# LSTM recurrence: products that stream their columns many times into unread PSUM

## The chip, the cores and the metric
One NeuronCore of a Trainium2 chip runs the whole kernel. The metric is the device time of one execution in microseconds. The kernel before took a median of 13971.03 us over 3 runs (13965.97 to 13977.05).

## What is computed
A graph network layer and a linear attention mix are added to x (6250 rows of 256); the result is normalised and goes through an LSTM with 256 state elements over all 6250 rows in order, batch 1. The part that the change touches is the LSTM:

```python
x_proj = jnp.einsum('btd,gd->btg', x, W_ih) + b_ih + b_hh
def step(carry, xp):
    h, c = carry
    gates = xp + h @ W_hh.T
    i, f, g, o = jnp.split(gates, 4, axis=-1)
    c = jax.nn.sigmoid(f) * c + jax.nn.sigmoid(i) * jnp.tanh(g)
    h = jax.nn.sigmoid(o) * jnp.tanh(c)
    return ((h, c), h)
```

Each step needs the state of the step before it, so the 6250 steps form one dependent chain.

## The kernel before
The kernel is a sequence of stages, each a block with one program for each engine. A normalisation of x, then a stage that gathers and scatters rows of the graph while TensorE computes the attention mix, then the feed-forward part of the graph network, its normalisation (products at lines 1161, 1170 and 1179), the recurrence (lines 1343 to 1564), and a last stage of running sums and output. The change is in the recurrence alone.

In the recurrence the 1024 gate rows are eight blocks of 128. Three gates (input, forget, cell) have two blocks each, m = 0 and 1, and collect in the PSUM regions gi[m][b]; the output gates collect in go[b]. b is one of two sets of banks: blocks of B = 5 steps alternate between them. So a region holds 5 steps, and for each step 3 gates with PARTS = 2 columns, 30 columns of the 512 of its bank, or 10 columns for the output gates. State, inputs and weights are split in two f16 parts each, so that three products (first part by first, first by second, second by first) replace one in f32. Each product is one load of 128x128 f16 weights (LDWEIGHTS) and one MATMUL with a moving operand of 1, 2, 5 or 10 columns.

TensorE's program of one step, in its order (`body`, from line 1434):
- `rest_of_weights`: 12 products of the weights' second parts with the state's first part, one column each. It waits for h1_ready of each half of the state.
- `weights` for m = 0: six products of the weights' first parts with both parts of the state, two columns, behind h2_ready of each half. The last signals ifg_made[0]. Then six for m = 1, and ifg_made[1].
- `output_gates`: 12 products of one column, then ogate_made.
- nine (or what is left) of the 44 products of `projection`, the input's share of the gates of the next five steps, written to the other set of banks. They have 5 or 10 columns: 6 x 5 for input, forget and cell gates and 2 x 7 for the output gates, the bias among them.


The other engines follow in a ring. VectorE sums the two parts of the gates (line 1538, once for each m), ScalarE takes tanh of them (line 1500, twice) and of the output gates (line 1505), VectorE makes the new cell (line 1542), ScalarE its tanh (line 1509), and VectorE writes the state's first part (line 1553, signals h1_ready) and its second (line 1558, h2_ready). Each engine works through its own queue in order; semaphores alone tie them together. SyncE moves the inputs in and the states out once in five steps. All products are issued by the helper at line 1422, so every one of them stands at that line in the profile:

```python
def matmul(to, w, v, start):
    return nc.tensor.matmul(to, w, v, start=start, stop=True, skip_group_check=True)
```

Of the kernel before, what the change touches and what calls it, by code (L numbers as in the profile page):

```python
# [33 lines left out]
KD = D // 128  # L34
# [18 lines left out]
B = 5  # L53
NB = N // B
NI = NB // 2
PARTS = 2
# [14 lines left out]
def due(count):  # L71


    return not isinstance(count, int) or count > 0
# [24 lines left out]
def gps_layer_kernel(nc, x, src, dst, gnn_eps, gW1, gb1, gW2, gb2, gamma, beta, w_qkv, b_qkv,  # L99
# [14 lines left out]
    with top, stage, nc.allow_non_contiguous_dma(reason="vectors of 256 numbers, loaded once"):  # L114
# [3 lines left out]
        def sb(name, shape, dt=F32, ctx=top):  # L118
            return ctx.enter_context(nc.sbuf_tensor(name, shape, dt))
# [6 lines left out]
        bank = [top.enter_context(nc.psum_tensor(f"bank{i}", [128, 512], F32)) for i in range(6)]  # L126
# [7 lines left out]
        whh = sb("whh", [128, PARTS, KD, G4], F16)  # L134
        wih = sb("wih", [128, PARTS, KD, G4], F16)
        gbias = sb("gbias", [128, G4], BF16)
# [30 lines left out]
        with ExitStack() as st:  # L167
# [15 lines left out]
            @block.sync  # L183
            def _(sp):
                xt, xnt = (v.rearrange("(p t) d -> p t d", p=R) for v in (x, xn_d))
                for j in range(XL):
                    at = slice(j * NT // XL, (j + 1) * NT // XL)
                    for lo, hi in SPLIT:
                        sp.dma_start(xall[lo:hi, at, :], xt[lo:hi, at, :]).then_inc(x_in[j], 16)
                for g in range(2):  # L190
                    for m, v in enumerate((src_g, dst_g)):
                        sp.dma_start(staged_i[:, g, m, :], v[g]).then_inc(staged[g], 16)
                sp.wait_ge(zeroed, 1)
                flat = [acc_d[a].rearrange("n d -> (n d)").rearrange("(p w) -> p w", p=128) for a in range(NA)]

                pieces = iter(range(NA * ZS))

                def zeros(count):
                    for _, piece in zip(range(count), pieces):
                        a, j = piece // ZS, piece % ZS  # L200
                        sp.dma_start(flat[a][:, j * ZW:(j + 1) * ZW], zero[:]).then_inc(zero_out[a], 16)

                zeros(ZEROS_AHEAD)
                for q in range(STORES):
                    at = slice(q * NT // STORES, (q + 1) * NT // STORES)
                    sp.wait_ge(xn_ready, (q + 1) * NT // STORES)
                    for lo, hi in SPLIT:
                        sp.dma_start(xnt[lo:hi, at, :], xall[lo:hi, at, :]).then_inc(xn_out, 16)
                    zeros(ZEROS_BETWEEN)
                zeros(NA * ZS - ZEROS_AHEAD - ZEROS_BETWEEN * STORES)  # L210
                sp.dma_start(x2_d[:, NB * KD * B * PARTS:], zero[:].bitcast(F16)[:, 0:2 * KD * B * PARTS]).then_inc(zero_out[NA - 1], 16)
                sp.wait_ge(xn_out, 32 * STORES)
# [1132 lines left out]
        with ExitStack() as st:  # L1345
            ones = sb("ones", [128, B], BF16, st)
            xs_ = sb("xsteps", [128, 2, PARTS, KD, B], F16, st)
            hp = sb("hp", [128, 2 * B, KD, 4], F16, st)
# [8 lines left out]
            gi = [[bank[2 * k + b][:, 0:B * 3 * PARTS].rearrange("p (t g c) -> p t g c", t=B, c=PARTS)  # L1357
                   for b in range(2)] for k in range(KD)]
            go = [bank[4 + b][:, 0:B * KD].rearrange("p (t m) -> p t m", t=B) for b in range(2)]

            def pair(name):
                return [sem(f"{name}{k}") for k in range(KD)]
# [12 lines left out]
            def steps(engine, body):  # L1375

                def blocks(i):
                    for b in range(2):
                        for s in range(B):
                            body(i * (2 * B) + (b * B + s), i, b, s)  # L1380

                first_apart(engine, NI, blocks)
# [20 lines left out]
            def projection(b):  # L1403

                for g in range(4):
                    for m in range(KD):
                        cols = slice((KD * g + m) * 128, (KD * g + m + 1) * 128)
                        if g == 3:
                            yield go[b][:, :, m], gbias[:, cols], ones[:], m == 0
                            for p, q in ((0, 0), (0, 1), (1, 0)):  # L1410
                                for k in range(KD):
                                    yield go[b][:, :, m], wih[:, p, k, cols], xs_[:, b, q, k, :], False
                        else:
                            to = gi[m][b][:, :, g, :]
                            yield to[:, :, 0:1], gbias[:, cols], ones[:].rearrange("p (t c) -> p t c", c=1), g == 0
                            for p in range(PARTS):
                                for k in range(KD):
                                    yield (to[:, :, 0:PARTS - p], wih[:, p, k, cols],
                                           xs_[:, b, 0:PARTS - p, k, :].rearrange("p c t -> p t c"), False)

            def matmul(to, w, v, start):
                return nc.tensor.matmul(to, w, v, start=start, stop=True, skip_group_check=True)  # L1422

            @block.tensor
            def _(pe):
                pe.wait_ge(lstm0, 1)
                pe.wait_ge(xs_in[0], 16)
                for m in projection(0):
                    last = matmul(*m)
                last.then_inc(x_proj, 1)  # L1430
                per_step = -(-(3 * KD * (1 + PARTS * KD) + KD * (1 + 3 * KD)) // B)
                state = {}

                def body(t, i, b, s):
                    if s == 0:
                        state["ahead"] = list(projection(1 - b))
                        pe.wait_ge(xs_in[1 - b], 16 * (i + 1 + b))
                    before = (b * B + s - 1) % (2 * B)

                    def product(to, p, k, g, m, at):  # L1440
                        cols = slice((KD * g + m) * 128, (KD * g + m + 1) * 128)
                        return matmul(to, whh[:, p, k, cols], hp[:, before, k, at], False)

                    FIRST, REST, BOTH = slice(3, 4), slice(2, 3), slice(2, 4)

                    def rest_of_weights(m, k):
                        for g in range(3):
                            product(gi[m][b][:, s, g, 0:1], 1, k, g, m, FIRST)

                    def weights(m, k):  # L1450
                        for g in range(3):
                            last = product(gi[m][b][:, s, g, :], 0, k, g, m, BOTH)
                        return last

                    def output_gates():
                        for m in range(KD):
                            to = go[b][:, s, m:m + 1]
                            for k in range(KD):
                                product(to, 1, k, 3, m, FIRST)
                                product(to, 0, k, 3, m, FIRST)  # L1460
                                last = product(to, 0, k, 3, m, REST)
                        return last

                    if due(t):
                        pe.wait_ge(h1_ready[0], t)
                    rest_of_weights(0, 0)
                    rest_of_weights(1, 0)
                    if due(t):
                        pe.wait_ge(h1_ready[1], t)
                    rest_of_weights(0, 1)  # L1470
                    rest_of_weights(1, 1)
                    if due(t):
                        pe.wait_ge(h2_ready[0], t)
                    weights(0, 0)
                    if due(t):
                        pe.wait_ge(h2_ready[1], t)
                    weights(0, 1).then_inc(ifg_made[0], 1)
                    weights(1, 0)
                    weights(1, 1).then_inc(ifg_made[1], 1)
                    output_gates().then_inc(o_made_, 1)  # L1480

                    n = per_step if s < B - 1 else len(state["ahead"])
                    for m in state["ahead"][:n]:
                        last = matmul(*m)
                    state["ahead"] = state["ahead"][n:]
                    if s == B - 1:
                        last.then_inc(x_proj, 1)

                steps(pe, body)

            @block.scalar
# [310 lines left out]
```

## Time and profile before

| | us |
|---|---|
| median of 3 runs | 13971.03 |
| profiled execution, its own time | 13987.69 |
| span of the profile | 13985.9 |
| TensorE busy with products | 10063.6 (72%) |
| TensorE busy with weight loads | 9131.5 (65%) |
| VectorE busy | 8604.1 (62%) |
| ScalarE busy | 5184.4 (37%) |
| mean granted clock of TensorE | 0.549 |

A busy share is the union of the records of an engine. A product's record lasts some 0.17 us, while the next one can start much earlier, so many overlap and a busy TensorE is not one at its peak. The granted clock is given as a share of 2.4 GHz: it has two levels, 1.0 and 0.5 (1.2 GHz). Times are in microseconds from the start of the span, except where a row gives a mean duration, which is in nanoseconds.

### The profile page before, as it was taken

The numbers are of one execution on the slowest core, as the hardware profiler recorded it, in microseconds if no ns is written. First come the engines' busy times: TensorE is split into PE (matmuls) and PEld (weight loads), VectorE is DVE, ScalarE is ACT, GpSimd is POOL, SyncE is SP. The second block draws the span as 40 slices with busy tenths as digits, with TensorE's granted clock in tenths as the row PEclk, the third lists the DMA queues.
The fourth block names the chain that finished last, engine by engine and source line by source line (L and its number), as shares of the span: only waits on it lengthen the run. The fifth ranks groups of instructions, "written<-read, shape, count | busy, mean of one in ns | idle before, by whom it ended". The sixth has DMA issues, their size and how long they took to land. (4 is left out here: it accounts for less than half of the span.)

```text
span 13985.9 us, 721250 instructions
## 1 busy us (share of the span) xinstructions
PE 10063.6 (72%) x285273; PEld 9131.5 (65%) x285273; DVE 8604.1 (62%) x65379; ACT 5184.4 (37%) x32393; POOL 2070.5 (15%) x1598
## 2 busy tenths in 40 slices
PE   3444444687777777777777777777777777777776
PEld 2333333567777777777777777777777777777775
DVE  4444222256666666666666666666666666666667
ACT  1111111144444444444444444444444444444443
POOL 5888788400000000000000000000000000000000
PEclk8666777865555555555555555555555555555556
DMA  6555455410000000000000000000000000000001
GB/s 164 91 90 90 80 83 83 92 34 1 1 1 1 1 1 1 1 1 1 1 1 1 1 1 1 1 1 1 1 1 1 1 1 1 1 1 1 1 1 19
DMA packets 2057504, 301.47 MB, mean 22 GB/s; under 512 B 1894943, under 2 KB 2013747, under 8 KB 2056843
## 3 DMA queue, kind: packets, MB, share of 16 engines
q0 software_dynamic: 150048, 204.90, 9.0%
q1 hardware_dynamic: 1896678, 91.09, 8.1%
q10 hardware_dynamic: 10742, 5.06, 0.1%
q8 instruction: 16, 0.26, 0.0%
q14 instruction: 20, 0.16, 0.0%
HBM read 153.07 MB, written 141.27 MB: 21 GB/s over the span
## 5 line engine op out<-in xcount | busy, mean ns | idle before, releaser
L1422 PE MATMUL bank<-hp,whh 128*128 128x1 f16 (+1 forms) x225000 | 7000.0, 166 | 2320.7 <-DVE hp L1553 2320.7
L1422 PEld LDWEIGHTS bank<-hp,whh 128*128 128x128 f16 x225000 | 6488.6, 104 | 2864.1 <-DVE hp L1553 2863.6
L1500 ACT ACTIVATE gates<-last_banks 128x3 f32<-128x3 f32 x12500 | 2085.4, 174 | 6161.2 <-DVE last_banks L1538 6161.2
L1538 DVE TENSOR_REDUCE last_banks<-bank 128x3 f32<-128x6 f32 x12500 | 2076.6, 172 | 2393.9 <-PE bank L1422 2393.9
L1422 PE MATMUL bank<-xsteps,wih 128*128 128x10 f16 (+1 forms) x45036 | 2331.0, 170 | 0.0
L1542 DVE CUSTOM_DVE_ANT_1 uv<-gates 128x4 f32<-128x4 f32 x12500 | 2019.4, 164 | 506.3 <-ACT gates L1500 0.2
L1553 DVE TENSOR_TENSOR_SCAN hp<-last_banks,opening 128x2 f16<-128x2 f32 x12500 | 1968.9, 161 | 569.1 <-ACT last_banks L1509 108.7
L1509 ACT ACTIVATE last_banks<-gates 128x1 f32<-128x1 f32 x12500 | 2085.2, 174 | 0.1
L1422 PEld LDWEIGHTS bank<-xsteps,wih 128*128 128x128 f16 x45036 | 1917.6, 104 | 0.0
L1558 DVE TENSOR_TENSOR_SCAN hp<-last_banks,hp 128x2 f16<-128x2 f32 x12500 | 1759.2, 159 | 0.0
L1629 POOL TENSOR_TENSOR U<-U (+1 forms) x25 | 27.5, 1139 | 11171.2 <-POOLq L1572 11171.2
L1422 PE MATMUL bank<-ones,gbias 128*128 128x5 bf16 x10008 | 1551.1, 168 | 9.4 <-DMA xsteps<-x_d 9.4
L385 POOL DMA_INDIRECT acc_d<-sums,target x782 | 1267.1, 1620 | 252.9 <-issue 204.7
L407 PE MATMUL bank<-rows,equal 128*128 128x256 f32 x1564 | 694.2, 622 | 778.0 <-DMA rows<-xn_d,staged_i 734.5
L407 PEld LDWEIGHTS bank<-rows,equal 128*128 128x128 f32 x1564 | 480.8, 322 | 927.3 <-issue 826.4
L1422 PEld LDWEIGHTS bank<-ones,gbias 128*128 128x128 bf16 x10008 | 1040.8, 104 | 9.7 <-issue 9.7
L1542 DVE DVE_READ_ACCUMULATOR2_ANT gates<- 128x1 f32 x12500 | 1038.5, 83 | 0.0
L1505 ACT ACTIVATE last_banks<-bank 128x2 f32<-128x2 f32 x6250 | 981.2, 157 | 0.0
L360 POOL DMA_INDIRECT rows<-xn_d,staged_i x782 | 774.7, 991 | 249.3 <-issue 215.9
L418 ACT ACTIVATE sums<-bank 128x512 f32<-128x512 f32 x391 | 212.1, 594 | 1587.2 <-PE bank L407 1583.0
L457 DVE TENSOR_TENSOR target<-dstf,move 128x4 int32<-128x4 f32 x196 | 32.0, 163 | 880.6 <-DMA acc_d<-sums,target 874.0
L644 PE MATMUL bank<-kvn 125*128 125x128 f32 x200 | 61.1, 461 | 482.7 <-DVE kvn L750 464.8
(184 smaller groups left out, 3199.8 us busy)
## 6 DMA issues: line engine op xcount, KB each, us to landing
xsteps<-x_d SPq DMA_DIRECT2D x1252, 5.0 KB, 1.8
U<-hp SPq DMA_DIRECT2D x1250, 5.0 KB, 2.5
acc_d<-zero SPq DMA_DIRECT2D x30, 640.0 KB, 12.9
ht<-acc_d SPq DMA_DIRECT2D x75, 224.0 KB
rows<-xn_d,staged_i POOLq DMA_INDIRECT x782
acc_d<-sums,target POOLq DMA_INDIRECT x782, 3.8
xi<-xn_d SPq DMA_DIRECT2D x50, 125.0 KB
xi<-in_x SPq DMA_DIRECT2D x50, 125.0 KB
```

The costliest lines, as they stand in the source:

```text
L360: pool.indirect_dma_start(out=rows[0:P, g, j, :], out_offset=None, in_=xn_d, in_offset=bass.IndirectOffsetOnAxis(ap=staged_i[0:P, g, 0, j: ...
L385: pool.indirect_dma_start(out=acc_d[a], out_offset=bass.IndirectOffsetOnAxis(ap=target[0:P, g, j:j + 1], axis=0), in_=sums[0:P, g, j, :], ...
L407: last = nc.tensor.matmul(prod[j // 2][0:P, j % 2, :], equal[0:P, g, j, 0:P], rows[0:P, g, j, :], start=True, stop=True)
L418: nc.scalar.activation(sums[0:P, g, 2 * m:2 * m + 2, :], prod[m][0:P], ACT.Copy)\
L1422: return nc.tensor.matmul(to, w, v, start=start, stop=True, skip_group_check=True)
L1500: nc.scalar.activation(gates[:, k, 0:6:2], zi[k], ACT.Tanh, scale=down)\
L1505: nc.scalar.activation(o_all, go[b][:, s], ACT.Tanh, scale=down).then_inc(o_act, 1)
L1509: nc.scalar.activation(o_tc[k][:, 1:2], gates[:, k, 5:6], ACT.Tanh).then_inc(tc_ready[k], 1)
L1538: nc.vector.tensor_reduce(zi[k], gi[k][b][:, s], axis=AX.X, op=ALU.add).then_inc(ifg_summed[k], 1)
L1542: nc.vector.tensor_tensor_reduce(out=uv[:, k, :].rearrange("p (a c) -> p a c", a=2), in0=gates[:, k, 0:4].rearrange("p (a c) -> p a c", a= ...
L1553: nc.vector.tensor_tensor_scan(hp[:, at, k, 2:4], o_tc[k], opening[:], RAISE, ALU.mult, ALU.subtract).then_inc(h1_ready[k], 1)
L1558: nc.vector.tensor_tensor_scan(hp[:, at, k, 0:3:2], o_tc[k], hp[:, at, k, 1:4:2], RAISE, ALU.mult, ALU.subtract).then_inc(h2_ready[k], 1)
```

## The change
Products write to wider regions. `gi_wide` and `go_wide` see the same banks as `gi` and `go`, but with the region repeated 16 times (30 columns each) and 48 times (10 columns each). Repetition 0 is what the other engines read, at the same place as before; the others are read by nobody. A product's moving operand is broadcast with a stride of zero, so that TensorE streams the same columns several times. The one-column products of `rest_of_weights` now have 16 columns, those of `weights` with k = 0 have 32 (with k = 1 still 2), those of `output_gates` 48, and those of `projection` 30. `spare_columns` is a product of 256 columns into the upper half of a bank of the set that is not being read; each step ends with two of them, and 48 precede step 0.

```diff
+            GATE_COLS, OUT_COLS = B * 3 * PARTS, B * KD
+            gi_wide = [[bank[2 * k + b][:, 0:GATE_COLS * 16].rearrange("p (j n) -> p j n", n=GATE_COLS) for b in range(2)]
+                       for k in range(KD)]
+            go_wide = [bank[4 + b][:, 0:OUT_COLS * 48].rearrange("p (j n) -> p j n", n=OUT_COLS) for b in range(2)]
+            NX = 6
+
+            def again(v, times):
+
+                return v.rearrange("p (o t) -> p o t", o=1).broadcast_to([128, times, v.shape[-1]])
...
-                            yield go[b][:, :, m], gbias[:, cols], ones[:], m == 0
+                            to = go_wide[b][:, 0:NX].rearrange("p j (t m) -> p j t m", m=KD)[:, :, :, m]
+                            yield to, gbias[:, cols], again(ones[:], NX), m == 0
...
-                                    yield go[b][:, :, m], wih[:, p, k, cols], xs_[:, b, q, k, :], False
+                                    yield to, wih[:, p, k, cols], again(xs_[:, b, q, k, :], NX), False
...
+                            to = gi_wide[m][b][:, 0:NX].rearrange("p j (t g c) -> p j t g c", g=3, c=PARTS)[:, :, :, g]
+                            yield to[:, :, :, 0], gbias[:, cols], again(ones[:], NX), g == 0
+                            for k in range(KD):
+                                both = xs_[:, b, 0:PARTS, k, :].rearrange("p c (o t) -> p o t c", o=1)
+                                yield (to[:, 0:NX // 2], wih[:, 0, k, cols],
+                                       both.broadcast_to([128, NX // 2, B, PARTS]), False)
+                            for k in range(KD):
+                                yield to[:, :, :, 0], wih[:, 1, k, cols], again(xs_[:, b, 0, k, :], NX), False
...
+                def spare_columns(b, start=False):
+
+                    return matmul(bank[2 + b][:, 256:512], wih[:, 0, 0, 0:128], whh[:, 0, 0, 0:256], start)
+
+                for n in range(48):
+                    spare_columns(1, start=n == 0)
...
-                        return matmul(to, whh[:, p, k, cols], hp[:, before, k, at], False)
+                        v = hp[:, before, k, at]
+                        return matmul(to, whh[:, p, k, cols], again(v, to.shape[1]) if len(to.shape) == 3 else v, False)
...
-                            product(gi[m][b][:, s, g, 0:1], 1, k, g, m, FIRST)
+                            product(gi_wide[m][b][:, :, col(s, g):col(s, g) + 1], 1, k, g, m, FIRST)
...
-                            last = product(gi[m][b][:, s, g, :], 0, k, g, m, BOTH)
+                            to = gi[m][b][:, s, g, :] if k else gi_wide[m][b][:, :, col(s, g):col(s, g) + PARTS]
+                            last = product(to, 0, k, g, m, BOTH)
...
-                            to = go[b][:, s, m:m + 1]
+                            to = go_wide[b][:, :, s * KD + m:s * KD + m + 1]
...
+                    for _ in range(2):
+                        last = spare_columns(1 - b)
```

TensorE, one step of the recurrence as it stood before (hp and whh are state and recurrent weights, xsteps and wih inputs and theirs, ones and gbias the bias):

```order
L1422 MATMUL bank<-hp,whh 128x1 x12
L1422 MATMUL bank<-hp,whh 128x2 x12
L1422 MATMUL bank<-hp,whh 128x1 x12
L1422 MATMUL bank<-xsteps,wih 128x5
L1422 MATMUL bank<-ones,gbias 128x5
L1422 MATMUL bank<-xsteps,wih 128x5 x6
```

TensorE, the same step after the change (the helper stands at line 1434 there):

```order
L1434 MATMUL bank<-hp,whh 128x16 x12
L1434 MATMUL bank<-hp,whh 128x16x2 x3
L1434 MATMUL bank<-hp,whh 128x2 x3
L1434 MATMUL bank<-hp,whh 128x16x2 x3
L1434 MATMUL bank<-hp,whh 128x2 x3
L1434 MATMUL bank<-hp,whh 128x48 x12
L1434 MATMUL bank<-xsteps,wih 128x30
L1434 MATMUL bank<-ones,gbias 128x30
L1434 MATMUL bank<-xsteps,wih 128x30 x6
L1434 MATMUL bank<-whh,wih 128x256 x2
```

The 36 products with the state keep their order; the two of 256 columns are the last of the step, ahead of the next step's first product in the queue.

## Rows read from the trace of the kernel before

**Rows 1.** The page: span, and the granted clock in 40 slices.
```profile
span 13985.9 us, 721250 instructions
...
PEclk8666777865555555555555555555555555555556
```

**Rows 2.** Stretches of stages: length, busy time and count by engine, granted clock.
```profile
core 0: us, PE busy (x) PEld busy (x) DVE busy (x) ACT busy (x) POOL busy (x), PEclk, DMA share, GB/s
2700.00:2860.00 160.00, 158.99 (x793) 141.66 (x793) 60.89 (x108) 54.76 (x132) 0.00 (x0) 1.00 0.31 93
2900.00:2985.00 85.00, 74.90 (x242) 53.89 (x242) 53.63 (x153) 42.59 (x83) 0.00 (x0) 0.50 0.14 52
...
5000.00:13000.00 8000.00, 6283.69 (x207033) 5881.75 (x207030) 5438.31 (x46215) 3446.91 (x23110) 0.00 (x0) 0.50 0.08 1
```

**Rows 3.** Waits of the recurrence, 5000 to 13000: us in total, times, longest.
```profile
DVE last_banks L1538 <- PE bank L1422: 1766.5, 4621, 0.4
PE bank L1422 <- DVE hp L1553: 1716.1, 4621, 0.5
```

**Rows 4.** Groups by form, 5000 to 13000: busy us, mean ns, idle before.
```profile
L1422 PE MATMUL bank<-hp,whh 128*128 128x1 f16 x110908 | 4336.3, 166 | 1716.1 <-DVE hp L1553 1716.1
...
L1553 DVE TENSOR_TENSOR_SCAN hp<-last_banks,opening 128x2 f16<-128x2 f32 x9243 | 1455.9, 161 | 420.8 <-ACT last_banks L1509 80.4
...
L1422 PE MATMUL bank<-xsteps,wih 128*128 128x10 f16 x11089 | 1057.6, 172 | 0.0
```

**Rows 5.** Timeline of one step: start us, us, engine, line, operation.
```profile
8000.12 0.16 ACT L1505 ACTIVATE last_banks<-bank 128x2 f32<-128x2 f32 x1
...
8000.26 0.33 ACT L1509 ACTIVATE last_banks<-gates 128x1 f32<-128x1 f32 x2
...
8000.47 0.32 DVE L1553 TENSOR_TENSOR_SCAN hp<-last_banks,opening 128x2 f16<-128x2 f32 x2
8000.68 1.04 PEld L1422 LDWEIGHTS bank<-hp,whh 128*128 128x128 f16 x36 [0.45 <-DVE hp L1553]
8000.69 1.12 PE L1422 MATMUL bank<-hp,whh 128*128 128x1 f16 x36 [0.36 <-DVE hp L1553]
8000.70 0.28 DVE L1558 TENSOR_TENSOR_SCAN hp<-last_banks,hp 128x2 f16<-128x2 f32 x2
8001.37 0.33 DVE L1538 TENSOR_REDUCE last_banks<-bank 128x3 f32<-128x6 f32 x2 [0.38 <-PE bank L1422]
```

**Rows 6.** Timeline, line 1170: eight one-column products, at clock 1.0, at 0.5.
```profile
2872.11 1.09 PE L1170 MATMUL bank<-small,csq 128*125 128x1 f32 x8
...
2879.39 1.84 PE L1170 MATMUL bank<-small,csq 128*125 128x1 f32 x8
```

**Rows 7.** Groups by form on TensorE: at clock 1.0, then at 0.5.
```profile
L1063 PE MATMUL bank<-hid,gw 128*128 128x250 f32 x364 | 80.8, 374 | 1.0 <-ACT U L1093 1.0
...
L1042 PE MATMUL bank<-ident,hsum 125*128 125x125 f32 x84 | 12.5, 270 | 0.0
...
L1170 PE MATMUL bank<-small,csq 128*125 128x1 f32 x8 | 1.1, 257 | 0.0
...
L1170 PE MATMUL bank<-small,csq 128*125 128x1 f32 x140 | 32.3, 351 | 0.1
L1179 PE MATMUL bank<-ident,nrs 125*128 125x125 f32 x34 | 11.2, 432 | 0.0
```

**Rows 8.** Scatter stage: a timeline piece, then stretches, columns as in rows 2.
```profile
332.60 3.55 PE L407 MATMUL bank<-rows,equal 128*128 128x256 f32 x8 [2.05 <-issue]
...
322.60:329.40 6.80, 3.34 (x19) 2.36 (x18) 2.58 (x6) 2.45 (x7) 5.27 (x6) 1.00 0.71 122
329.40:332.80 3.40, 1.35 (x7) 0.72 (x6) 3.19 (x8) 0.00 (x0) 2.90 (x2) 1.00 0.28 83
332.80:336.20 3.40, 3.36 (x8) 2.10 (x7) 2.70 (x5) 0.64 (x2) 2.99 (x2) 0.50 0.68 65
336.20:339.60 3.40, 0.00 (x0) 0.00 (x0) 0.00 (x0) 1.08 (x2) 2.79 (x3) 1.00 0.61 65
```

More of the change, by code:

```diff
@@ L1408, in projection @@
                         if g == 3:
-                            yield go[b][:, :, m], gbias[:, cols], ones[:], m == 0
+                            to = go_wide[b][:, 0:NX].rearrange("p j (t m) -> p j t m", m=KD)[:, :, :, m]
+                            yield to, gbias[:, cols], again(ones[:], NX), m == 0
                             for p, q in ((0, 0), (0, 1), (1, 0)):
                                 for k in range(KD):
-                                    yield go[b][:, :, m], wih[:, p, k, cols], xs_[:, b, q, k, :], False
+                                    yield to, wih[:, p, k, cols], again(xs_[:, b, q, k, :], NX), False
                         else:
[L1414 to L1419, printed above, removed]
+                            to = gi_wide[m][b][:, 0:NX].rearrange("p j (t g c) -> p j t g c", g=3, c=PARTS)[:, :, :, g]
[6 more added lines that the diff above has]
+                                yield to[:, :, :, 0], wih[:, 1, k, cols], again(xs_[:, b, 0, k, :], NX), False
             def matmul(to, w, v, start):
@@ L1441, in product, with col @@
                         cols = slice((KD * g + m) * 128, (KD * g + m + 1) * 128)
-                        return matmul(to, whh[:, p, k, cols], hp[:, before, k, at], False)
+                        v = hp[:, before, k, at]
+                        return matmul(to, whh[:, p, k, cols], again(v, to.shape[1]) if len(to.shape) == 3 else v, False)
+                    def col(s, g):
+                        return (s * 3 + g) * PARTS
                     FIRST, REST, BOTH = slice(3, 4), slice(2, 3), slice(2, 4)
```

## The prediction
> **What bounds the kernel now.** The page is read first: the span, and the row of the granted clock [rows 1]. It averages 0.6 to 0.8 in the first nine slices and stands at 0.5 from the tenth to the end of the recurrence. That is the lower of the engine's two levels, 1.2 GHz, for three quarters of the span. Stretches by stage say it sharply [rows 2]: 5000 to 13000 us is one uniform stretch at 0.50. The scan of line 1553 runs twice a step and stands 9243 times in those 8000 us [rows 4], so a step takes 8000 / 4621.5 = 1.731 us, and the 6250 steps take 10.8 ms.
>
> The waits of that stretch [rows 3] show a ring with no engine full. VectorE waits for TensorE 1766.5 / 4621 = 0.38 us a step, and TensorE for VectorE 0.37 us. The timeline of one step gives the ring [rows 5]: scan at .47, first weight load at .68, first product at .69, first reduction at 1.37, and so on through VectorE and ScalarE to the next scan. Of its 1.731 us, 0.68 us (.69 to 1.37) is TensorE's: it is the time from the first product to the reduction that needs the 18th. The 36 products of the ring start within 1.12 - 0.166 us, so one follows another at 0.954 / 35 = 0.0273 us [rows 4, 5]. A product with 10 columns lasts 6 ns longer than one with 1, and its neighbours follow no later. So it is the load of 128x128 weights ahead of each product that sets this pace, not the columns.
>
> **The change, part by part.** A step has 104 columns now: 12 + 24 + 12 of the state, and 280 of the inputs spread over five steps. After it: 12x16 for the first parts, 2x(3x32 + 3x2) for both parts, 12x48 for the output gates, 264 for inputs (44 products of 30 columns over five steps), 512 for the two spare products. Together 1748. The number of products on the ring, their order and all waits stay. Added are two products and two loads at the end of each step, and 48 products before step 0. VectorE, ScalarE and SyncE get nothing new, and nothing they read gets wider.
>
> **Does the clock rise, and hold?** At 1.2 GHz a column takes 0.83 ns, so the new step would stream 1.45 us of columns, against 0.09 of 1.73 us now. What the trace shows of the clock: with 250-column products back to back the level was 1.0 [rows 2, 7]; with TensorE busy 88% of the time, but mostly on 1-column products, it was 0.50 [rows 2, 7], and it is 0.50 in the recurrence. So neither having records nor having no long gap is enough; streamed columns differ. The 48 products are 12,288 columns on end, and I expect 1.0 within them, as it rose in the scatter stage after a stretch at 0.5 in which products of 256 columns kept the engine busy for 3.36 of 3.40 us [rows 8]. Holding is the doubtful half. At 2.4 GHz the step streams 1748 x 0.417 ns = 0.73 us of about 1.65, 44%. In the scatter stage the level stayed at 1.0 over 6.80 us in which wide products kept the engine busy 3.34 us, and fell after a stretch with 1.35 us of 3.40 [rows 8]. The new step stands nearer to the first. I take it that it holds.
>
> **What a full clock is worth.** The nearest rows for the pace are one-column products with a full weight load at both levels [rows 6, 7]: eight in 1.84 us at 0.5 give (1.84 - 0.351) / 7 = 0.213 us each, eight in 1.09 us at 1.0 give (1.09 - 0.257) / 7 = 0.119. Ratio 0.56, so 0.0273 becomes 0.015 us. These loads are f32, ours f16; the other end is no gain, 0.0273. I take 0.015, because these rows too are set by the load. Seventeen such paces would save 0.21 us, but the ring has a second edge. The products with the new state's second half (the 16th on) wait for the scan pair of line 1558, which ends at .98 [rows 5]. From a scan's end to the load it releases are 0.05 us (.63 to .68 [rows 5]). So the 16th product can come at about 1.03 + 0.02 = 1.05, and now it comes at .69 + 15 x 0.0273 = 1.10. That gives 0.05 us, and the two paces after it 2 x 0.012 = 0.024: **0.075 us a step**.
>
> The time from a product's start to its result may fall too. For one column nothing does, once the pace is taken off: 0.351 - 0.213 = 0.138 and 0.257 - 0.119 = 0.138 [rows 6, 7]. For 125 columns, 432 ns at 0.5 and 270 at 1.0, columns taken off (208 and 104), 224 and 166 are left [rows 7]: 0.058 less, of which a part is the wait of the first of a pair, so I bound it by 0.05. The ring's products ahead of the reduction have two columns, nearest to one: I take 0, and keep 0.05 for the range. The Trainium skill ("TensorE: Matmul & The Clock Gate", "Single matmul latency") has a single product's latency fall from (219+N)/1.2 to (398+N)/2.4 ns; for N = 1 that is an estimated 17 ns, and the sum would be 106 us lower by it. The rows of one column show none of it.
>
> The second half of the gates gets its reduction six paces after the first, 0.09 for 0.16 us, but it follows VectorE and ScalarE behind the first half and sets nothing; I cost it at nothing. Widening at full clock costs nothing either: a 48-column product streams 0.020 us, its results are wanted by line 1505, which stands 0.14 us ahead of line 1509 in ScalarE's queue [rows 5]; 12 x 0.020 is still less than the 12 x 0.0273 it takes now. The two spare products take 512 x 0.417 = 0.21 us and lie in TensorE's idle 0.37 us. TensorE's own sum, 24 x 0.015 + 12 x 0.020 + 9 x 0.015 + 0.21 = 0.95 us, is far under the step, so its queue is empty when the scan comes. If that cover goes (at half clock), see the first rival. The 48 products cost between 48 x 0.107 = 5 and 48 x 0.213 = 10 us, once: 8.
>
> Sum: 6250 x 0.075 = 469, less 8, 461 us. The profiled execution took 13987.69 us (span 13985.9), the median of the runs is 16.7 us lower at 13971.03; the same difference is expected after. 13971 - 461 = **13510 us**.
>
> **Rivals.**
> The clock falls, or never rises (slower). The place is the output gates. At 1.2 GHz a 48-column product takes 0.040 us, not 0.0273: twelve end 0.15 us later, and their own columns add 0.04. Line 1505 comes 0.19 us later, and line 1509, which stands behind it on ScalarE and on the ring 0.14 us after it with a 0.16 us operation between [rows 5], comes about 0.17 later. TensorE alone gives a lower bound: 24 x 0.0273 + 12 x 0.040 + 9 x 0.0273 + 0.427 = 1.81 us, 0.08 more than the step. Per step +0.17: 6250 x 0.17 = 1060, **15030 us**. For it: 44% of columns is no dense stream, and 2900 to 2985 shows a busy engine at 0.5. Against it: at half clock the step would be filled with columns to 1.45 of 1.90 us, so a fall would tend to be followed by a rise. It decides from the point where a share f of steps at half clock has 0.17 f > 0.075 (1 - f): f over 0.31.
>
> The clock is full, but the pace hardly moves. Pairs of load and product then keep some 0.027 us, and what is left is 0 to 0.05 us a step of latency; the middle, 0.02, gives 6250 x 0.02 - 8 = 117 us less, **13854 us**. For it: no f16 load at 1.0 stands in this trace. Against it: the f32 rows. The Trainium skill states such a floor ("TensorE: Matmul & The Clock Gate", "Wait — 56ns, not 53.3ns?"): starts never closer than about 25 ns at full clock, however few the columns. By that page 17 x 0.0023 = 0.039 us a step would be saved, an estimate of 13735 us; the trace has 0.0273 at half clock and cannot show the floor.
>
> The change does not do what it says: the columns don't count as work for the clock, but the step has room for them. There is none at half clock (1.81 us against 1.731), so this ends in the first rival.
>
> **How the numbers follow.** Clock full and pace shortened: 0.52. Clock full and pace kept: 0.22. Clock at half for over a third of the steps: 0.20. Gain and loss about cancelling (f near 0.31): 0.06. A measurement here tells 0.2%, 28 us. The forecast's bounds are 0.125 us a step (0.075 + 0.05), which is 13971 - 781 + 8 = 13198, and about 0.05, 13665. The range goes from 13230 to 13900, to the far side of the second case, and leaves the slow case out. Faster 0.75: the first two cases, and a little of the last. Same 0.04, slower 0.21.
>
> **What would show it.** Right: PEclk 1.0 from 3000 us to the end; a step of 1.65 us; 36 ring products in 0.7 to 0.9 us instead of 1.12; VectorE's wait for TensorE 0.30 us a step instead of 0.38; the gaps between reduction, tanh, cell and scan unchanged. Pace kept: PEclk 1.0, but the first 18 products still in 0.46 us. Wrong: PEclk at 0.5 or mixed, line 1505's successor further from the reduction, and TensorE without idle time.

## The result, and the profile after

The changed kernel takes **14772.03 us** (median of 4 runs, 14764.79 to 14774.01) against 13969.15 of the kernel before in the same comparison: a ratio of 1.0573, 95% interval 1.0555 to 1.0591. It is 5.7% slower, 803 us. The forecast was 13510 us, faster, with a range to 13900.

The page of the changed kernel, its span, the granted clock, and one of its groups (busy us, mean ns, idle time before it and what ended it):

```profile
span 14771.7 us, 746346 instructions
...
PEclk8666777799999999999999999999999999999998
...
L1531 ACT ACTIVATE last_banks<-bank 128x2 f32<-128x2 f32 x6250 | 981.2, 157 | 1078.2 <-PE bank L1434 1078.2
```

The clock is what was forecast: 0.9 or more from the ninth slice to the last but one, where it was 0.5 from the tenth on [rows 1]. Stretches of it, columns as in [rows 2]:

```profile
3000.00:3010.00 10.00, 9.83 (x210) 8.65 (x209) 3.56 (x34) 2.19 (x17) 0.00 (x0) 1.00 0.01 2
...
5000.00:13000.00 8000.00, 7693.34 (x201653) 6494.99 (x201651) 4714.97 (x43090) 2812.12 (x21545) 0.00 (x0) 1.00 0.07 1
```

It is 1.00 from the first steps and for the whole recurrence, not 0.50. So the 803 us are lost at full clock.

The waits (us in total, times, longest) and the groups by form of the stretch from 5000 to 13000:

```profile
DVE last_banks L1564 <- PE bank L1434: 1825.1, 4309, 0.4
...
DVE hp L1579 <- ACT last_banks L1535: 1070.2, 4309, 0.3
ACT last_banks L1531 <- PE bank L1434: 743.3, 4309, 0.2
```

```profile
L1434 PE MATMUL bank<-hp,whh 128*128 128x48 f16 x51708 | 2983.1, 206 | 0.0
L1434 PE MATMUL bank<-hp,whh 128*128 128x16 f16 x51708 | 2071.2, 179 | 306.7
...
L1434 PE MATMUL bank<-hp,whh 128*128 128x2 f16 x25848 | 1563.8, 163 | 0.0
...
L1579 DVE TENSOR_TENSOR_SCAN hp<-last_banks,opening 128x2 f16<-128x2 f32 x8618 | 1085.3, 161 | 1070.2 <-ACT last_banks L1535 1070.2
```

The scan of line 1579 (1553 before) stands 8618 times, so a step takes 8000 / 4309 = 1.857 us, 0.1255 more than the 1.731 before; 6250 x 0.1255 = 784 us, which is the difference of the spans (14771.7 - 13985.9 = 785.8). Two waits of the table are new. ScalarE's line 1531 (1505 before), the tanh of the output gates, now waits 743.3 / 4309 = 0.17 us a step for TensorE, and the scan waits 1070.2 / 4309 = 0.25 us for ScalarE, where line 1553's wait was 80.4 us in all [rows 4]. The timeline of a step:

```profile
8001.48 1.32 PE L1434 MATMUL bank<-hp,whh 128*128 128x16 f16 x36
8002.14 0.32 DVE L1564 TENSOR_REDUCE last_banks<-bank 128x3 f32<-128x6 f32 x2 [0.42 <-PE bank L1434]
8002.34 0.32 ACT L1526 ACTIVATE gates<-last_banks 128x3 f32<-128x3 f32 x2 [1.02 <-DVE last_banks L1564]
...
8002.84 0.16 ACT L1531 ACTIVATE last_banks<-bank 128x2 f32<-128x2 f32 x1 [0.17 <-PE bank L1434]
...
8002.91 0.26 ACT L1535 ACTIVATE last_banks<-gates 128x1 f32<-128x1 f32 x2
8003.11 0.25 DVE L1579 TENSOR_TENSOR_SCAN hp<-last_banks,opening 128x2 f16<-128x2 f32 x2 [0.24 <-ACT last_banks L1535]
```

Set beside [rows 5]: from the first product to the first reduction it is 0.66 us (.48 to 2.14), 0.02 less than the 0.68 before. But the 36 products of the ring take 1.32 us instead of 1.12. Line 1531 starts at 2.84, 0.70 after the reduction; before, that was 0.48 (1.37 to 0.12 of the next step, 1.73 us on [rows 5]). Line 1535 (1509 before), the tanh of the cell, must follow it on ScalarE's queue and does so 0.07 us later. The ring loses there more than it wins at its start.

How much a 48-column product takes comes from the same row. The first 24 products need 24 x 0.0257 = 0.62 us (the reduction behind the 18th shows that pace: 0.66 less the 0.2 from a product's start to its reader is 0.46 for 18). The twelve of the output gates take the rest: 1.32 - 0.206 - 0.62 = 0.49 over 11 starts, **0.045 us each**, where I had put 0.020.

### The profile page after: what moved, and what is told of

Read it like the earlier page. It is cut to its first block and busy times, and to the rows that moved or that the text cites. A ratio compares the mean times of both kernels' runs of the same rounds, so it can differ in the third digit from the quotient of the medians.

```text
span 14771.7 us, 746346 instructions
## 1 busy us (share of the span) xinstructions
PE 12730.3 (86%) x297821; PEld 10604.7 (72%) x297821; DVE 8088.8 (55%) x65379; ACT 4602.0 (31%) x32393; POOL 2067.4 (14%) x1598
## 5 line engine op out<-in xcount | busy, mean ns | idle before, releaser
L1434 PEld LDWEIGHTS bank<-hp,whh 128*128 128x128 f16 x225000 | 7346.7, 96 | 2182.6 <-DVE hp L1579 2182.2
L1434 PE MATMUL bank<-hp,whh 128*128 128x16 f16 (+2 forms) x225000 | 8267.0, 185 | 444.7 <-DVE hp L1579 0.2
L1434 PE MATMUL bank<-xsteps,wih 128*128 128x30 f16 x45036 | 2506.8, 190 | 0.0
L1579 DVE TENSOR_TENSOR_SCAN hp<-last_banks,opening 128x2 f16<-128x2 f32 x12500 | 1574.1, 161 | 1552.2 <-ACT last_banks L1535 1552.2
L1434 PE MATMUL bank<-whh,wih 128*128 128x256 f16 x12548 | 2385.7, 272 | 0.0
L1434 PEld LDWEIGHTS bank<-xsteps,wih 128*128 128x128 f16 x45036 | 2007.1, 97 | 0.0
L1434 PE MATMUL bank<-ones,gbias 128*128 128x30 bf16 x10008 | 1712.6, 190 | 8.7 <-DMA xsteps<-x_d 8.7
L1535 ACT ACTIVATE last_banks<-gates 128x1 f32<-128x1 f32 x12500 | 1617.4, 167 | 0.0
L1584 DVE TENSOR_TENSOR_SCAN hp<-last_banks,hp 128x2 f16<-128x2 f32 x12500 | 1596.7, 164 | 0.0
L1434 PEld LDWEIGHTS bank<-whh,wih 128*128 128x128 f16 x12548 | 784.6, 97 | 1.2
```

Source lines behind the costliest of these rows:

```text
L1535: nc.scalar.activation(o_tc[k][:, 1:2], gates[:, k, 5:6], ACT.Tanh).then_inc(tc_ready[k], 1)
L1579: nc.vector.tensor_tensor_scan(hp[:, at, k, 2:4], o_tc[k], opening[:], RAISE, ALU.mult, ALU.subtract).then_inc(h1_ready[k], 1)
L1584: nc.vector.tensor_tensor_scan(hp[:, at, k, 0:3:2], o_tc[k], hp[:, at, k, 1:4:2], RAISE, ALU.mult, ALU.subtract).then_inc(h2_ready[k], 1)
```

## The experiments

Theory 1: the loss is the output gates' twelve products alone, because of something in how their 48 columns are read or written. Theory 2: it is spread, and goes with the number of columns a step streams, or with the spare products.

**What form of product is slow.** Twelve forms stand ahead of step 0, where the clock is already 1.0, twelve products of each on end, each with its own weight load. The number of columns is the label.

```diff
+                form(side[:, 0:40], whh[:, 0, 0, 0:40])
+                form(side[:, 0:44].rearrange("p (j n) -> p j n", n=1), again(state1, 44))
+                form(stepped(46), whh[:, 0, 0, 0:46].rearrange("p (j n) -> p j n", n=1))
+                form(stepped(48), again(state1, 48))
+                form(side[:, 0:42].rearrange("p (j n) -> p j n", n=1), whh[:, 0, 0, 0:42 * 4].rearrange("p (j n) -> p j n", n=4)[:, :, 0:1])
+                for n in (2, 8, 16, 24, 32):
+                    form(stepped(n), again(state1, n))
+                form(side[:, 0:24 * 10].rearrange("p (j n) -> p j n", n=10)[:, :, 0:2], again(whh[:, 0, 0, 0:2], 24))
+                form(side[:, 0:56], whh[:, 0, 0, 0:56])
```

(`stepped(n)` is n columns of PSUM that stand 10 apart, as in the changed kernel's output gates.)

> Eleven forms of product, twelve of each on end, stand after the 48 products and before step 0, at full clock. They tell whether the 44 ns from one 48-column product to the next come from reading one column over and over (stride 0) or from writing columns 10 apart. Theory 1, the read: 44 columns read with stride 0 and written side by side follow at about 0.93 x 44 = 41 ns, 46 columns read side by side and written apart at 25 ns or less. Theory 2, the write: the other way round, 25 and about 43 ns. 48 with both as in the changed kernel: 44 ns. 40 columns side by side on both: 25 ns, the floor that the two-column products show. Of the apart forms 2, 8, 16 and 24 columns 25 ns, 32 about 30 ns. 24 pairs (48 columns): under 30 ns if pairs move at full rate. The whole kernel: as the changed one, 14772 us plus about 5.

The whole kernel took 14778.08 us. Its groups by form, busy us and mean ns, from 3003.5 to 3008:

```profile
L1434 PE MATMUL bank<-whh,wih 128*128 128x46 f16 x12 | 0.7, 216 | 0.0
L1434 PE MATMUL bank<-whh,wih 128*128 128x44 f16 x12 | 0.6, 202 | 0.0
L1434 PE MATMUL bank<-whh,wih 128*128 128x42 f16 x12 | 0.6, 212 | 0.0
L1434 PE MATMUL bank<-whh,wih 128*128 128x32 f16 x12 | 0.5, 193 | 0.0
L1434 PE MATMUL bank<-whh,wih 128*128 128x24 f16 x12 | 0.5, 184 | 0.0
...
L1434 PE MATMUL bank<-whh,wih 128*128 128x40 f16 x12 | 0.5, 180 | 0.0
L1434 PE MATMUL bank<-whh,wih 128*128 128x56 f16 x11 | 0.4, 187 | 0.0
```

The stretch of the 24 pairs, and that of the 48 columns one by one:

```profile
L1434 PE MATMUL bank<-whh,wih 128*128 128x48 f16 x12 | 0.5, 183 | 0.0
```

```profile
L1434 PE MATMUL bank<-whh,wih 128*128 128x48 f16 x10 | 0.6, 208 | 0.0
```

A product of two columns lasts 163 ns in the ring at this clock, so the excess over it, divided by the number of columns, gives the price of a column. Columns side by side on both sides: 40 last 180 and 56 last 187, 0.43 ns each, the full rate. 24 pairs 10 apart: 183, 0.42. Forms whose columns are handled one by one: 44 last 202 (0.9), 46 last 216 (1.2), 48 last 208 (0.9), 42 last 212 (1.2), 24 last 184 (0.9). The ends of such records are modelled by the profiler; the starts are not, and they say the same. Products of 40 or 56 columns and of 24 pairs start 25 to 26 ns apart, those of 44, 46, 48 and 42 lone columns 41, 40, 45 and 39 ns, which is 0.9 ns a column throughout, and those of 8 to 24 lone columns 26.6 ns. Neither of my two theories on reading and writing held alone: 44 was written side by side and is slow, 46 was read side by side and is slow. But 44 and 46 both were given as rows of one element, so these forms leave open whether place or shape is what counts.

**Reading and writing apart.** Seven more forms, each with a plain single run where it can have one.

```diff
+                form(side[:, 0:50], state1.broadcast_to([128, 50]))
+                form(side[:, 0:52], apart(52, 2))
+                form(side[:, 0:54], apart(54, 8))
+                form(side[:, 0:2 * 36].rearrange("p (n j) -> p n j", j=2)[:, :, 0], many[:, 0:36])
+                form(side[:, 0:2 * 30].rearrange("p (j n) -> p j n", n=2), state1.rearrange("p (o t) -> p o t", o=1).broadcast_to([128, 30, 2]))
+                form(side[:, 0:2 * 31].rearrange("p (j n) -> p j n", n=2), again(many[:, 0:2], 31))
+                form(side[:, 0:58], many[:, 0:58])
```

> Seven more forms ahead of step 0, twelve products of each, at full clock, to split the reading side and the writing side. Durations over the 163 ns of a two-column product, per column: 0.43 ns is full rate, 0.9 or more is slow. If reading with stride 0 is slow in itself: 50 columns of one element with a single stride of 0 last 163 + 45 = 208 ns, and 60 columns of it written in pairs 217 or more. If only the shape (an inner run of one) was slow: 185 and 189. Columns read 2 elements apart (4 bytes), 52 of them: 185 if two in the same 16 bytes suffice, as the Trainium skill ('SBUF — State Buffer', 'Door 1: The DMA port swizzle') states; 210 if every column that is no neighbour is slow. 54 read 8 apart (16 bytes): slow, 212 or more. 36 columns written 2 apart (8 bytes), read side by side: slow, 163 + 36 x 1.15 = 204. 62 columns as 31 pairs: 190. 58 side by side: 188.

The whole kernel took 14769.46 us. Groups by form ahead of step 0:

```profile
L1434 PE MATMUL bank<-whh,wih 128*128 128x54 f16 x12 | 1.4, 278 | 0.0
L1434 PE MATMUL bank<-whh,wih 128*128 128x36 f16 x12 | 0.6, 201 | 0.0
L1434 PE MATMUL bank<-whh,wih 128*128 128x62 f16 x12 | 0.5, 191 | 0.0
L1434 PE MATMUL bank<-whh,wih 128*128 128x60 f16 x12 | 0.5, 191 | 0.0
L1434 PE MATMUL bank<-whh,wih 128*128 128x58 f16 x12 | 0.5, 188 | 0.0
L1434 PE MATMUL bank<-whh,wih 128*128 128x52 f16 x12 | 0.5, 186 | 0.0
L1434 PE MATMUL bank<-whh,wih 128*128 128x50 f16 x12 | 0.5, 183 | 0.0
```

Reading one element over and over is not slow: 50 columns of it last 183 ns and 60 last 191, close to the full rate. So the 44 of the kernel above were slow by their shape, a pattern whose inner run is one element, though the addresses were adjacent. Both their sides had that shape; which of the two counts was not tested. Reading 2 elements apart costs nothing (52 last 186), as the Trainium skill ("SBUF — State Buffer", "Door 1: The DMA port swizzle") has it for two hits on 16 bytes; reading 16 bytes apart costs most (54 last 278, and start 98 ns apart, 1.8 ns a column). Writing is the other half: 36 columns written 2 apart last 201 with a plain read, and start 34 ns apart, 0.94 ns each. The Trainium skill says so for PSUM ("PSUM — Partial Sum Buffer", "Specifications (TRN2)"): its lines are 8 bytes, two f32 values, and any non-contiguous pattern slows products. Lone columns at half the rate agree with it. The pairs do not: they too are non-contiguous, and go at full rate; there the measurement decides. The changed kernel's output gates had both faults, copies 10 apart and rows of one.

**The output gates narrow.**

```diff
-                            to = go_wide[b][:, :, s * KD + m:s * KD + m + 1]
+                            to = go[b][:, s, m:m + 1]
```

> The output gates' twelve products take one column again, all else as changed (1184 columns a step). Theory 1, they alone are the loss: if the clock holds at 1.0, the step is 1.731 - 0.024 = 1.707 us and the time about 13830; if it falls to 0.5, TensorE needs 45 x 0.027 + 0.43 = 1.63 us, just under the old step, and the time is 13980 to 14100. Theory 2, the loss is spread (spare products in the way, slower access to PSUM): over 14300 at clock 1.0.

13899.61 us, ratio to before 0.9946 (0.9930 to 0.9963). One line turns 803 us of loss into 72 us of gain: theory 1, and not theory 2, since the two spare products, the 16- and 32-column products and the wide inputs are all still there. Stretches, columns as in [rows 2]:

```profile
3000.00:3100.00 100.00, 91.16 (x2702) 75.09 (x2701) 65.35 (x570) 41.17 (x285) 0.00 (x0) 1.00 0.08 3
5000.00:13000.00 8000.00, 7375.32 (x217881) 6102.08 (x217877) 5367.96 (x46557) 3385.93 (x23280) 0.00 (x0) 0.93 0.08 1
```

At 1184 columns a step the clock holds 1.00 at first and averages 0.93 later, and the time lies 50 and 55 us above the two kernels that follow, which hold it. The time that I had expected for a clock that holds, 13830 us, was therefore missed.

**Gates of 24 columns, and gates of one, with four spare products.** Edit: `go_wide[b][:, 0:24, ...]` or `go[b]` for the gates, and in both

```diff
-                    for _ in range(2):
+                    for _ in range(4):
```

> Output gates with 24 columns instead of 48, and four spare products instead of two (1972 columns a step, more than the changed kernel's 1748). Theory 1, only a product longer than the 25 ns pace costs, and spare products fit into TensorE's idle time: clock 1.0, output gates at 25 ns each, step 1.71 us, time about 13840. Theory 2, columns cost wherever they are: at least as slow as the changed kernel, 14770.

> Output gates with one column and four spare products (1696 columns a step, near the changed kernel's 1748). If total columns alone decide the clock, it holds at 1.0 as there and the time is about 13830. If it falls, four spare products at half clock make TensorE the bound: 45 x 0.027 + 0.85 = 2.07 us a step, about 16000 us.

13849.50 us (ratio 0.9910, 0.9893 to 0.9926) and 13844.94 us (0.9907, 0.9891 to 0.9924), both at clock 1.00 from 5000 to 13000. The first streams 1972 columns a step, more than the changed kernel, and is 6% faster than it. So columns cost nothing where TensorE is idle, and next to nothing where they stay under the pace: the twelve products of 24 lone columns start 26.6 ns apart instead of 25.0, which the ring's slack hides.

**Gates of 40 columns.** Edit: `go_wide[b][:, 0:40, ...]`, two spare products as in the change.

> The changed kernel with output gates of 40 columns instead of 48 (1652 columns a step). If a lone column costs 0.93 ns and the ring has 0.06 us of slack at line 1531: twelve products at 37 ns are 12 x 10.7 = 0.13 us later than at 26.5, less the slack 0.07 us a step, 6250 x 0.07 = 430 over the kernel with 24 columns (13850): 14280. If the loss went with the number of columns in the step, it would be near the changed kernel's: 14700.

14276.93 us, ratio 1.0216 (1.0199 to 1.0233). The timeline of a step:

```profile
8000.19 1.24 PE L1434 MATMUL bank<-hp,whh 128*128 128x16 f16 x36
8000.85 0.32 DVE L1564 TENSOR_REDUCE last_banks<-bank 128x3 f32<-128x6 f32 x2 [0.42 <-PE bank L1434]
...
8001.47 0.16 ACT L1531 ACTIVATE last_banks<-bank 128x2 f32<-128x2 f32 x1
...
8001.54 0.26 ACT L1535 ACTIVATE last_banks<-gates 128x1 f32<-128x1 f32 x2
```

The 36 products end 1.24 us after the first starts, line 1531 starts 0.62 after the reduction, and line 1535 again 0.07 behind it. The time is the one worked out (14280): a lone column costs 0.93 ns, 12 products of them delay line 1531, and beyond 0.06 us of slack the ring pays all of it. From 40 to 48 columns the time rises by 495 us, which is 0.079 us a step or 0.83 ns for each of the 12 x 8 columns.

**The same 48 columns side by side.** Copies of an output gate stand next to it, not 10 apart, and are read as one run; the inputs' products of the output gates follow the new places.

```diff
-            go = [bank[4 + b][:, 0:B * KD].rearrange("p (t m) -> p t m", t=B) for b in range(2)]
-            go_wide = [bank[4 + b][:, 0:OUT_COLS * 48].rearrange("p (j n) -> p j n", n=OUT_COLS) for b in range(2)]
+            go_wide = [bank[4 + b][:, 0:B * KD * 48].rearrange("p (t m j) -> p t m j", m=KD, j=48) for b in range(2)]
+            go = [go_wide[b][:, :, :, 0] for b in range(2)]
...
-                            to = go_wide[b][:, :, s * KD + m:s * KD + m + 1]
+                            to = go_wide[b][:, s, m, :]
...
+                        if len(to.shape) == 2 and to.shape[1] == 48:
+                            v = v.broadcast_to([128, 48])
```

> The changed kernel with the output gates' 48 copies side by side in PSUM instead of 10 columns apart; the same 1748 columns, products, loads and waits in the same order. The forms showed 50 columns side by side read with stride 0 at 25 ns a product, and 0.93 ns a column when each stands alone. If the place of the columns is the loss: the twelve products follow at 25 ns, clock 1.0, step 1.708 us, 13845 as with narrow gates. If the loss goes with the number of columns: 14770.

13854.35 us, ratio 0.9913 (0.9896 to 0.9929). Stretch, one group and timeline:

```profile
5000.00:13000.00 8000.00, 7242.12 (x218963) 5942.93 (x218960) 5369.70 (x46784) 3440.61 (x23393) 0.00 (x0) 1.00 0.08 1
```

```profile
L1438 PE MATMUL bank<-hp,whh 128*128 128x48 f16 x56148 | 2141.7, 183 | 0.0
```

```profile
8000.55 1.08 PE L1438 MATMUL bank<-hp,whh 128*128 128x16 f16 x36 [0.23 <-DVE hp L1585]
8001.20 0.32 DVE L1570 TENSOR_REDUCE last_banks<-bank 128x3 f32<-128x6 f32 x2 [0.41 <-PE bank L1438]
...
8001.67 0.16 ACT L1537 ACTIVATE last_banks<-bank 128x2 f32<-128x2 f32 x1
...
8001.82 0.32 ACT L1541 ACTIVATE last_banks<-gates 128x1 f32<-128x1 f32 x2
```

Same 1748 columns, same products, same order: the 48-column product lasts 183 ns, not 206, 36 products take 1.08 us, not 1.32, line 1531 starts 0.47 after the reduction, and the time falls by 918 us. This shows the cause: how the copies are laid out and handed over, not how many they are. The edit changed two things at once, the place in PSUM and the shape of the patterns; the forms ahead of step 0 showed each of them slow by itself.

**The first twelve products narrow too.** On the kernel with narrow gates and four spare products, and on the one with copies side by side:

```diff
-                            product(gi_wide[m][b][:, :, col(s, g):col(s, g) + 1], 1, k, g, m, FIRST)
+                            product(gi[m][b][:, s, g, 0:1], 1, k, g, m, FIRST)
```

> The kernel with narrow output gates and four spare products, and the first twelve products of the ring with one column again (1516 columns a step). Theory 1 (25 ns is the floor, 26.5 ns the pace of columns read and written one by one): 11 paces ahead of the 18th product shorten by 1.5 ns, the step from 1.708 to about 1.692 us, time 13750, clock 1.0. Rival: the wait for the state's second part sets the 16th product, and nothing is gained: 13845. If the clock falls: over 14500.

> The same, and the ring's first twelve products with one column again (1568 columns a step, two spare products). They go from 26.5 to 25 ns: step 1.692 us, 13750, as the kernel with narrow gates, narrow first products and four spare products (13753). If 1568 columns do not hold the clock, between 13750 and 13990.

13753.40 us (ratio 0.9840, 0.9824 to 0.9857) and **13751.25 us** (0.9841, 0.9825 to 0.9857): 1.6% faster than before, with clock 1.00. The two can't be told apart by their times, and are the best of the study. Of the second, the products and the reduction:

```profile
8000.52 1.07 PE L1438 MATMUL bank<-hp,whh 128*128 128x1 f16 x36 [0.16 <-DVE hp L1585]
...
8001.16 0.32 DVE L1570 TENSOR_REDUCE last_banks<-bank 128x3 f32<-128x6 f32 x2 [0.35 <-PE bank L1438]
```

36 starts at (1.07 - 0.183) / 35 = 0.0253 us, and 0.64 from first product to reduction. With 16 lone columns these twelve products had cost 1.3 ns more each: the twelve cover 15 ns more in the traces, and the two edits gained 92 and 103 us, 15 to 17 ns a step.

**Is the widening needed for the clock?** The kernel before with the 48 products ahead and two spare products a step, nothing widened (616 columns a step):

> The kernel before, with nothing widened, but with the 48 products ahead and the two spare products a step (616 columns a step). If the widened products are needed for the clock: it falls to 0.5 after the start, the two spare products take 0.43 us of TensorE's idle time, 45 x 0.027 + 0.43 = 1.65 us is under the step, and the time is 13980 to 14050. If the spare products alone hold it: clock 1.0, every pace 25 ns, 13740.

13986.03 us (median of 10 runs), ratio 1.0006 (0.9996 to 1.0016): no clear difference from before. The medians lie 8.7 us apart, about what the 48 products take there (7.7 us in the trace).

```profile
3000.00:3010.00 10.00, 9.60 (x242) 8.01 (x241) 4.61 (x42) 2.80 (x20) 0.00 (x0) 0.83 0.02 3
3010.00:3030.00 20.00, 19.96 (x537) 15.08 (x534) 13.68 (x119) 8.95 (x60) 0.00 (x0) 0.50 0.08 5
5000.00:13000.00 8000.00, 7997.54 (x216264) 6128.25 (x216262) 5438.10 (x46210) 3447.26 (x23105) 0.00 (x0) 0.50 0.08 1
```

The clock comes up in the start and is at 0.50 soon after, and stays there. At half clock two spare products hide in TensorE's idle time. The widened products are needed; and full clock is worth 13986 - 13751 = 235 us on this ring, 0.038 us a step.

**Are the 48 products ahead needed?** The changed kernel with one instead of 48:

> The changed kernel with one product ahead of step 0 instead of 48. If the steps raise the clock by themselves (1.45 of some 1.9 us filled with columns at half clock), it is 1.0 a few steps after the start and the time is the changed kernel's less 5 to 8 us, 14765. If they cannot, the clock stays at 0.5: output gates at 45 ns or more and the spare products at 213 ns each, over 15000.

14772.84 us, the same as with them (ratio to before 1.0567, 1.0550 to 1.0585).

```profile
2998.00:3003.00 5.00, 4.94 (x126) 4.60 (x124) 1.28 (x12) 0.77 (x7) 0.00 (x0) 0.71 0.02 1
3003.00:3006.00 3.00, 2.89 (x78) 2.33 (x75) 1.86 (x18) 1.13 (x9) 0.00 (x0) 1.00 0.02 5
5000.00:13000.00 8000.00, 7692.08 (x201658) 6493.79 (x201654) 4715.39 (x43088) 2813.40 (x21545) 0.00 (x0) 1.00 0.07 1
```

TensorE's timeline there, of the inputs' first product, of steps 0 and 1:

```profile
2997.83 0.21 PE L1434 MATMUL bank<-ones,gbias 128*128 128x30 bf16 x1 [9.16 <-DMA xsteps<-x_d]
...
2999.94 1.49 PE L1434 MATMUL bank<-hp,whh 128*128 128x16 f16 x36
...
3001.96 1.32 PE L1434 MATMUL bank<-hp,whh 128*128 128x16 f16 x36
```

The clock rises without the 48: it is at 1.0 before the end of step 0, after 2.1 us of the inputs' 30-column products on end and 1 us of the step, and step 1 has the 1.32 us of the changed kernel. So they don't help. What they cost is too little for the times to show, since the four runs of either kernel spread over 8 to 9 us. It shows in the changed kernel's trace, where the inputs came 3.0 us earlier:

```profile
2994.82 0.21 PE L1434 MATMUL bank<-ones,gbias 128*128 128x30 bf16 x1 [8.75 <-DMA xsteps<-x_d]
...
2996.74 6.72 PE L1434 MATMUL bank<-whh,wih 128*128 128x256 f16 x48
3003.30 1.31 PE L1434 MATMUL bank<-hp,whh 128*128 128x16 f16 x36
```

In the changed kernel the ring starts 6.56 us after the first of the 48, and from the inputs' first product to the ring's last it takes 6.2 us longer than here. I had put 5 to 10.

## Why the prediction was wrong

**The step that failed** is in the part on full clock: "Widening at full clock costs nothing either: a 48-column product streams 0.020 us". It streams 0.045 us. I took 0.417 ns a column from the clock level for every product, without asking whether a column 10 f32 values from the next is written as fast as one beside it. The rows of before held no product of more than 10 columns in the recurrence, and I gave this price no upper bound; the Trainium skill states the rule for PSUM in the section named above, and I had not weighed it. With 0.93 ns a column in the sum, and the pace of 0.0265 us that lone columns have at least, it would have been 12 x (0.045 - 0.0265) = 0.22 us later at line 1531, less 0.07 of slack, 0.15 us a step. The measured loss is 0.148 us (1.857 less the 1.709 of the kernel with 24 columns).

**The chain behind it was named, at the wrong place.** The first rival has it: the output gates late, line 1505 late, line 1509 behind it on ScalarE. I tied it to half clock alone. That its cost of 0.17 us a step was near the measured 0.148 is luck: it came from 0.83 ns a column at half clock, where the loss comes from lone columns at full clock. One size in it was off: I counted line 1509 to follow 0.14 us after line 1505 at best; it follows after 0.07, and that is the slack of 0.06 to 0.07 which the kernel with 40 columns confirms.

**The clock: right.** It rises and holds through the whole recurrence. Of the kernels here those with 1516 to 1972 columns a step stood at 1.00 from 5000 to 13000, 1184 at 0.93, 616 at 0.50. The first rival's condition, a clock at half, did not come about. The 48 products ahead cost 6.6 us where I had put 8.

**The worth of full clock: over-sized by a factor of two to three.** I forecast 0.075 us a step from a pace that would fall from 0.0273 to 0.015, as the f32 rows do [rows 6]. It falls to 0.0253, with one column or with 48 side by side. The ring's 18 products gain 0.02 us in the changed kernel and 0.04 with its first twelve narrow, and the second edge I saw, the wait for the state's second part, is not reached: in the best kernel the 16th product comes 15 x 0.0253 = 0.38 us after the first, and the scans that write the second part (line 1558 before) end 0.28 us after it. So what happened to the pace is my second rival, "the pace hardly moves". Its 13854 us is met by the kernel with copies side by side (13854.35) by luck, since it put all its gain into latency and none into the pace; the nearer one is the estimate from the floor of about 25 ns that the Trainium skill states ("TensorE: Matmul & The Clock Gate", "Wait — 56ns, not 53.3ns?"), 13735 us, which is 0.1% from the 13751 of the best kernel. The trace agrees: 0.0253 us with one column, and the same with 48 side by side.

**A product's latency** was put at no change, and that holds to 2 or 3 ns: one column lasts 166 ns at 0.5 [rows 4] and 164 at 1.0 (the last two kernels), and from the start of the 18th product to the reduction it is 0.203 us before and 0.200 after (middle values of over 100 steps). The 17 ns that the prediction estimates in its part on latency do not show.

**Right besides**: spare products in TensorE's idle time cost nothing at either level (four of them at 1.0, two at 0.5), and the unchanged engines keep their distances: the reduction to the tanh of the gates is 0.20 us in the changed kernel, 0.21 with copies side by side.

## What to carry to other kernels

A product's cost is not its number of columns alone: columns that stand alone, in PSUM or as rows of one element in an access pattern, cost about 0.9 ns instead of 0.42, so padding must be laid side by side, as one run. Padding on products that someone waits for must stay under the pace that they have anyway. What doesn't fit there goes into the engine's idle time, as wide products. And before paying for a full clock, ask what is bound by it: here the products were bound by a pace that the clock hardly moves, 0.0273 to 0.0253 us, so all of it was worth 235 us of 13986 here.

## What the hardware showed that I had not expected

- A load of 128x128 f16 weights with a narrow product follows the one before at 0.0273 us at 1.2 GHz [rows 5] and 0.0253 at 2.4 GHz. Up to 56 columns side by side ride along at full clock for 1 ns or less (25.7 ns from start to start).
- A pattern whose inner run is one element is slow even where its addresses are adjacent: 44 columns so last 202 ns, 50 in one run 183, read with stride 0 both times.
- Read 16 bytes apart, 54 columns last 278 ns and start 98 ns apart, 1.8 ns a column; 4 bytes apart 52 last 186.
- A clock at 0.5 was raised with one 256-column product ahead instead of 48, after 2.1 us of 30-column products and 1 us of the first step (the kernel with one product ahead).

What stays open: how a shape with rows of one element and a distance of 10 share the cost of the output gates' products, since each alone already costs all of it, and which side of a product the shape slows.
